# The place one-hots of the last sort, made in eight one-input column instructions in place of two wide two-input ones

## What is computed

```
h = relu(layernorm(x))
x = x + relu(relu((h*(1+eps) + segment_sum(h[src], dst)) @ W1 + b1) @ W2 + b2)      # layer one
h = relu(layernorm(x))
x = x + h @ w_self.T + scatter_add over edges e, at row src[e], of h[dst[e]] @ W_rel[type[e]]   # layer two
```

## Time and profile before

| what | value |
|---|---|
| three runs | 1236.69 us median (1233.98 to 1239.51) |
| the profiled execution | 1234.93 us, its span 1233.1 us |
| busy, share of the span | PE 73%, DVE 58%, ACT 30%, POOL 68% |
| last sort beside sort 2's groups | 409 to 618 us after the span's start |
| groups 47 to 51, end of layer one's sums | 622 to 642 us |
| dense part and products, first gather of layer two | 642 to 692 us |

### The profile page before, as it was taken

One profiled execution on the slowest core, in us unless ns is written; L12 is line 12 of the kernel. 1 busy time (PEld: TensorE's weight loads), 2 busy tenths in 40 slices (PEclk: granted clock), 3 DMA queues, 4 the chain that ended last, 5 costly groups with the idle time before them and its releaser, 6 DMA issues.

```text
span 1233.1 us, 13150 instructions
## 1 busy us (share of the span) xinstructions
PE 897.0 (73%) x3799; PEld 571.9 (46%) x3799; DVE 718.0 (58%) x2165; ACT 372.5 (30%) x945; POOL 834.9 (68%) x833
## 2 busy tenths in 40 slices
PE   4777848978744899999959998965655655655654
PEld 2443424434312577777634433844444444444443
DVE  7896569857578899999935432833222323322331
ACT  7444314635300588888804432000000000000001
POOL 0177757778777777777740475777777777777772
PEclk9688878989986899999968999977777777677677
DMA  4443323433342334334333898212122122121224
GB/s 100 121 134 113 108 61 101 135 105 100 107 110 75 106 105 133 110 105 138 107 49 121 264 299 266 54 52 54 52 54 54 51 54 53 52 53 52 53 54 73
DMA packets 50307, 122.86 MB, mean 100 GB/s; under 512 B 16156, under 2 KB 27021, under 8 KB 47487
## 3 DMA queue, kind: packets, MB, share of 16 engines
q0 software_dynamic: 33088, 67.82, 21.8%
q1 hardware_dynamic: 16844, 52.62, 13.5%
q10 hardware_dynamic: 308, 1.60, 0.5%
HBM read 71.86 MB, written 50.10 MB: 99 GB/s over the span
## 4 chain that ended last, share of the span: by engine, by line
POOL 25%; issue 9%; PE 8%; SPq 4%; DVE 2%; DMA 2%; ACT 0%; POOLq 0%; DVEq 0%; ACTq 0%
POOL gathered L423 25%; SPq L382 4%; PE ps L999 3%; PE ps L1081 2%; DMA gathered<-z_table,row_of 1%; DVE spare L890 1%; PE ps L1058 1%; PE ps L1048 1%; PE ps L1095 0%; DMA z_table<-spare 0%; DMA gathered<-h_table,row_of 0%; PE ps L1003 0%; DVE x_sb L920 0%; ACT spare L519 0%; DVE stats L580 0%
## 5 line engine op out<-in xcount | busy, mean ns | idle before, releaser
L423 POOL DMA_INDIRECT gathered<-h_table,row_of x416 | 443.7, 1067 | 187.7 <-issue 120.1
L423 POOL DMA_INDIRECT gathered<-z_table,row_of x410 | 388.6, 948 | 190.4 <-issue 120.0
L999 PE MATMUL ps<-node_hot,gathered 128*128 128x250 f32 x820 | 279.7, 511 | 170.7 <-DMA gathered<-z_table,row_of 170.7
L806 DVE TENSOR_SCALAR node_hot<-iota_f,key_of 128x250 f32<-128x250 f32 x410 | 153.8, 379 | 294.3 <-PE ps L999 286.1
L999 PEld LDWEIGHTS ps<-node_hot,gathered 128*128 128x128 f32 x820 | 208.1, 262 | 242.1 <-issue 207.0
L1003 PE MATMUL ps<-node_hot,gathered 128*128 128x506 bf16 (+1 forms) x1248 | 243.8, 350 | 75.9 <-DMA gathered<-h_table,row_of 57.6
L1003 PEld LDWEIGHTS ps<-node_hot,gathered 128*128 128x128 bf16 x1248 | 126.5, 103 | 179.4 <-issue 112.1
L498 ACT ACTIVATE place_val_b<-place_hot,code_b 125x128 f16<-125x128 f16 x400 | 173.8, 520 | 100.5 <-DVE place_hot L733 100.3
L490 ACT ACTIVATE scratch<-scratch,code_b 125x208 f16<-125x208 f16 (+1 forms) x328 | 114.4, 430 | 177.3 <-DVE scratch L758 177.3
L545 ACT COPY spare<-ps 128x500 f32<-128x500 f32 (+1 forms) x7 | 3.1, 563 | 459.8 <-PE ps L999 459.8
L972 PE MATMUL ps<-scratch,place_val_a 125*128 125x410 f16 x400 | 138.3, 346 | 2.6 <-DVE scratch L743 2.4
(11 more groups left out here) (170 smaller groups left out, 541.8 us busy)
## 6 DMA issues: line engine op xcount, KB each, us to landing
z_table<-spare SPq DMA_DIRECT2D x50, 448.0 KB
z_table<-zeros_z SPq DMA_DIRECT2D x19, 896.0 KB
gathered<-h_table,row_of POOLq DMA_INDIRECT x416
gathered<-z_table,row_of POOLq DMA_INDIRECT x410, 2.5
z_table<-spare SPq DMA_DIRECT2D x50, 52.0 KB
z_table<-zeros_z SPq DMA_DIRECT2D x19, 104.0 KB
out<-x_sb SPq DMA_DIRECT2D x6, 224.0 KB
h_table<-gathered SPq DMA_DIRECT2D x1, 1092.0 KB
```

Of the source, the lines that this page charges most:

```text
L423: pool.indirect_dma_start(place if s == LAST else place.rearrange("p j d -> p (j d)"), None, z_table if s == LAST else h_table, bass.Indir ...
L806: V.tensor_scalar(node_hot_of[s][:, k % HOTS[s], :], (iota_f if s == LAST else iota_h)[:, 0:WIDE[s]], key_of[s][:, k:k + 1], None, ALU.is_ ...
L999: last = T.matmul(psf[:, bass.ds(offs[i], WIDE[s])], rows, node_hot_of[s][:, k % HOTS[s], :], start=False, stop=False, skip_group_check=True)
```

## The change

In the last sort alone, `place_hot` and `place_val_a` of a batch are no longer made by two wide instructions. A new array `place_code_a`, which takes the memory of `place_val_a` with each column contiguous, is made column by column on DVE: one tensor input (`iota_h`), two per-partition scalars (`place_f`, `code_f1`), `is_equal` then `mult`. Each raises `code_ready`. ACT scales that column, in place of the 0/1 one, by what is now the low code divided by the high code. PE reads `place_code_a` for its first matmul. In `rank_place` two instructions (lines 711 and 712) are replaced by five, with a reciprocal among them; the high code has its zero moved so that it can be divided by. `read_last` takes the place of `read_sorted`, with two more DVE instructions. In the diff below the first `sort_last` is ACT's, the second DVE's; the block `if s == LAST` stands in `rank_place`, ahead of lines 711 and 712. The sorts before, PE's and ACT's instruction counts, the gathers and all of layer two's other work stay.

```
+        place_code_a = place_val_a[:, :, :, :].rearrange("p u v b -> p u (v b)").rearrange("p u (b v) -> p u b v", b=BATCH)
+        place_f, code_f1 = src_i.bitcast(F32), dst_i.bitcast(F32)
...
+            def sort_last(batch, buf):
+                for i in range(BATCH):
+                    act.wait_ge(code_ready, batch * BATCH + i + 1)
+                    nc.scalar.activation(place_val_b[:, buf, i, :], place_code_a[:, buf, i, :], ACT.Copy,
+                                         scale=code_b[1][:, batch * BATCH + i:batch * BATCH + i + 1]).then_inc(val_ready, 1)
...
-                own(V.tensor_copy(place_h[l][:, cs], scr1))
+                own(V.tensor_copy(place_f[:, :] if s == LAST else place_h[l][:, cs], scr1))
...
+                if s == LAST:
+                    own(V.tensor_scalar(code_f1[:, :], scr0, HALF_CODE, None, ALU.is_ge))
+                    own(V.scalar_tensor_tensor(code_f1[:, :], scr0, -HALF_CODE, code_f1[:, :], ALU.add, ALU.add))
+                    own(V.tensor_scalar(scr1.bitcast(F32), scr1, -HALF_CODE, 1.0 / CODE, ALU.add, ALU.mult))
+                    own(V.reciprocal(code_b[1][:, :], code_f1[:, :]))
+                    own(V.tensor_tensor(code_b[1][:, :], code_b[1][:, :], scr1.bitcast(F32), ALU.mult))
+                    return
...
+            def sort_last(s, batch, buf):
+                dve.wait_ge(batch_used, batch + (BATCHES_BEFORE[s] + 1))
+                for i in range(BATCH):
+                    c = batch * BATCH + i
+                    V.tensor_scalar(place_code_a[:, buf, i, :], iota_h[0:EP, 0:P], place_f[:, c:c + 1], code_f1[:, c:c + 1],
+                                    ALU.is_equal, ALU.mult).then_inc(code_ready, 1)
+                for i in range(BATCH):
+                    c = batch * BATCH + i
+                    last = V.tensor_scalar(chunk_hot[:, buf, i, 0:CHUNKS[s]], iota_h[0:EP, 0:CHUNKS[s]],
+                                           chunk_f[1][:, c:c + 1], None, ALU.is_equal)
+                last.then_inc(batch_ready, 1)
+
+            def read_last():
+                w = CHUNKS[LAST]
+                above, value = (scratch[:, i * WIDEST:i * WIDEST + w] for i in (1, 2))
+                dve.wait_ge(batch_used, BATCH_BUFS + BATCHES_BEFORE[LAST] + COLS[LAST] // BATCH)
+                own(V.tensor_scalar(above, ps[:, 7, 0:w], 0.25, None, ALU.is_ge))
+                own(V.scalar_tensor_tensor(value, ps[:, 7, 0:w], 0.0, above, ALU.add, ALU.subtract))
+                V.tensor_scalar(s0[:, 0:w], value, HALF_CODE + 0.5, CODE, ALU.add, ALU.mult).then_inc(sorted_read, 1)
+                dve.wait_ge(sorted_read, LAST + 1)
...
-                    T.matmul(ps[:, 7, 0:w], place_val_a[:, buf, :, i], hot, start=False, stop=False, skip_group_check=True)
+                    T.matmul(ps[:, 7, 0:w], place_code_a[:, buf, i, :] if s == LAST else place_val_a[:, buf, :, i], hot, start=False, stop=False, skip_group_check=True)
```

More of the change, by code:

```diff
@@ L229, in build @@
         place_ready, pair_ready = sem("place_ready"), sem("pair_ready")
-        batch_ready = sem("batch_ready")
+        batch_ready, code_ready = sem("batch_ready"), sem("code_ready")
         val_ready, val_a_ready = sem("val_ready"), sem("val_a_ready")
@@ L499, in sort_batch @@
                                          scale=code_b[l][:, c0 + batch * BATCH + i:c0 + batch * BATCH + i + 1]).then_inc(val_ready, 1)
-            for s in range(1, NSORT):
-                batches_alone(s, sort_batch if s == LAST else sort_pair, 0, COLS[s] // BATCH)
+            for s in range(1, LAST):
+                batches_alone(s, sort_pair, 0, COLS[s] // BATCH)
+            def sort_last(batch, buf):
[3 more added lines that the diff above has]
+                                         scale=code_b[1][:, batch * BATCH + i:batch * BATCH + i + 1]).then_inc(val_ready, 1)
+            for b in range(COLS[LAST] // BATCH):
+                sort_last(b, (BATCHES_BEFORE[LAST] + b) % BATCH_BUFS)
             def z_odd_copies(tiles):
@@ L864, in _ @@
                     dve.wait_ge(nhot_used, CHUNKS_BEFORE[s - 1])
-                groups_beside(s - 1, node_hots, sort_batch if s == LAST else sort_pair)
+                groups_beside(s - 1, node_hots, sort_last if s == LAST else sort_pair)
                 if s == LAST:
-                    read_sorted(s)
+                    read_last()
                 else:
```

## The result

The changed kernel takes **1283.98 us**, median of three runs (1283.56 to 1284.23), against 1236.69 us: ratio 1.0382, 95% interval 1.0344 to 1.0419. The profiled execution took 1283.56 us, its span is 1281.8 us, 48.7 us longer than before. The direction was forecast; the 1253 us and the range up to 1264 were not large enough.

A forecast was written before the change was run, and what follows sets the result against it. DVE, PE and POOL almost level in the last sort, DVE setting the pace; DVE's 18.0 + 4.2 + 1.0 = 23.2 us, past 5.0 us of slack, moves the end +18.2: 1234.93 + 18.2 = 1253 us, range 1242 to 1264.

The forecast's parts named there:

- DVE's price of the change: Last sort: eight place instructions at 1.81 us replace two wide ones at 1.45, 50 batches, +18.0 us of DVE.
- the code preparation: DVE ahead of the first node one-hot: five instructions with a reciprocal replace lines 711 and 712, +4.2 us.
- The estimate from the Trainium skill: Place one-hots on DVE: 0.094 us each, 0.75 us for eight, saving 35 us; the forecast used the trace row instead.
- The 5.0 us of slack: End of layer one: DVE and PE may be 5.0 us later against POOL before the end moves.
- what follows from group 47: End of layer one: group 47 added at 648.2, group 51's gathers start then instead of 629.98, end moves +18.2 us.
- The forecast's own range: Main case, chance 0.80: 1244 to 1262 us, from reciprocal, landing, per-instruction price and interference.
- ACT and PE at 0: Last sort: ACT's 3.49 us and PE's 4.08 us a step are covered by DVE's 4.48, cost 0.
- POOL at 0: Gathers beside the last sort: most of 21.4 us lost to wide instructions may go, but credit 0, POOL waits for PE.
- rival C: Last sort: an unbroken run of one-input DVE instructions starves gathers; at a 1.35 us mean, 1273 us; chance 0.07.
- Its decision point, 1.217 us: Mean gather beside the last sort above which gather starvation decides the time: 1.092 + 18.2 / 146 us.

The follow-up runs named there:

- e2: Changed kernel with each batch's place and chunk one-hots in turns of one, nothing added or left out; 1254.66 us, ratio 1.0124.
- e4: Kernel before plus an unused tensor_reduce, 0.32 us of DVE, in each of the last sort's 50 batches; 1253.90 us, ratio 1.0121.
- e9: Changed kernel with place and chunk one-hots in turns of two; 1269.57 us, ratio 1.0228.
- e7: Changed kernel with place and chunk one-hots in turns of four; 1277.48 us, ratio 1.0320.
- e3: Changed kernel with DVE waiting for its own signal once a batch, behind the eight place one-hots; 1265.42 us, ratio 1.0211.
- e5: Changed kernel with a small POOL memset ahead of each of sort 2's gathers, to move their phase; one run, 1290.43 us.
- e8: Kernel before with a next-group node one-hot after every two pair one-hots in sorts 1 and 2, last sort unchanged; 1218.34 us, ratio 0.9831.

## Why the prediction was right and wrong

- **DVE's price of the change: right.** Eight place one-hots take 504.48 - 502.70 = 1.78 us (forecast 1.81, removed 1.45); the step is 4.45 us (about 4.48). By these steps, DVE's cost is 50 x (4.45 - 4.12) = 16.5 us, not 18.0; in e2, where DVE is the bound throughout, first to last batch takes 222.6 us in place of 202.7, so 19.8 us. The 18.0 lies between. DVE's timeline ahead of the sort has the code preparation:

```profile
407.11 0.37 DVE L725 TENSOR_SCALAR dst_i<-t 125x400 f32<-125x400 int32 x1
407.51 0.61 DVE L726 SCALAR_TENSOR_TENSOR dst_i<-t,dst_i 125x400 f32<-125x400 int32 x1
408.15 0.49 DVE L727 TENSOR_SCALAR t<-t 125x400 f32<-125x400 int32 x1
408.68 2.65 DVE L728 RECIPROCAL code_b<-dst_i 125x400 f32<-125x400 f32 x1
411.37 0.57 DVE L729 TENSOR_TENSOR code_b<-code_b,t 125x400 f32<-125x400 f32 x1
411.98 0.87 DVE L849 TENSOR_SCALAR node_hot<-iota_h,key_of 128x250 bf16<-128x250 f16 x4
```

  411.98 - 407.11 = 4.87 us in place of 0.68: +4.2, as forecast. The estimate from the Trainium skill, "VectorE: DVE Perf Modes", section "The TRN2 errata — SBUF-src ops pay a fixed extra latency per instruction", 0.094 us for a place instruction, was far too low: 0.22 measured.
- **The 5.0 us of slack and what follows from group 47: right**, shown by e4 (22.0 us of DVE move group 51's gathers by 16.4) and e2 (POOL waits for PE, gathers at 650.26 for 648.2).
- **The forecast's own range** does not add up: -1, -2, -2 and -3 below and +9 and +3 above 1253 give 1245 to 1265, not 1244 to 1262. Nothing hangs on it.
- **ACT and PE at 0: right.** ACT falls from 42 to 28 us of 50, with the columns contiguous; the granted clock is 1.00 from 450 to 550 us, and 0.95 from 550 to 620, where DVE and PE wait.
- **POOL at 0: this step failed.** "POOL gains only lead" was written because the wide two-input instructions were the only thing that I saw stop a gather. Mean gathers were to come down to near 1.0 us; they went up to 1.425. That the replacement could hold gathers longer than what it replaced was in the sum at nothing, and only in rival C. With this, POOL ends 144 x 0.333 = 48 us later, past the 18.2 us that DVE needs, so POOL decides alone. Where the order of DVE's instructions lets gathers in, the forecast's 1253 us appears (e2).
- **Rival C had the mechanism, at a chance of 0.07 and a mean of 1.35 us, 1273 us.** Its decision point, 1.217 us, held: mean gathers of 1.324, 1.378 and 1.430 us (e9, e7, the change, all 412 to 640 us) go with 1270, 1277 and 1284 us, while 1.022 leaves DVE the bound. The row that should have weighed more is in the earlier trace rows: 1.2 us lost to seven one-input instructions. I set it against narrower runs that cost gathers little, without knowing why they did. POOL's timeline of the kernel before has, beside the chunk one-hots that start at 482.35:

```profile
482.71 1.03 POOL L423 DMA_INDIRECT gathered<-h_table,row_of  x1 [0.30 <-issue]
```

  It comes to end 1.31 us into the run, a moment at which the changed kernel holds gathers, and is 0.09 us late; 33 gathers of the kernel before come to end 1.30 to 1.32 us into it, and none is later than that. So the calm beside these runs belonged to a step with the wide instructions and the pauses in it, and said nothing of a step without them. What I also left out is that a periodic DVE step and the gathers lock to each other (2.90 and 0.95 us in turn, step after step), so that a meeting that was rare before comes in every step.
- By the Trainium skill, "SBUF — State Buffer", section "Who interferes with whom", a one-input DVE instruction such as `tensor_scalar` can also hold the port pair that it shares with GpSimd, for the whole instruction. I had cited only that section's sentence on two inputs. The traces agree that a run of one-input instructions holds a gather, but not on for how long: 1.96 us, through eight instructions and four more, not one of 0.24 us. Whether these instructions take that pair no trace here shows.

**What stays open.** When a gather is held. In the changed kernel 61 gathers come to end inside the chunk one-hots: those 0.35 to 1.38 us into them are held, 36 in all, those up to 0.33 or from 1.49 us on are not, so the moment matters. In e3 such moments hold none, and in the kernel before none at 1.30 to 1.32 us, so a pause ahead of the run matters, or the wait for a semaphore that comes with it, and why is not known. What keeps long holds out of the kernel before, the wide instructions, the pause between them or the moment, was not separated. e5 was to move the phase and did not. 51 gathers of the changed kernel come to end in its runs of eight place one-hots and none is held there, while runs of four of them (e7) hold 22 of 50. Whether "kind" is the width, the number of scalars, the output's type or the program's line was not separated. Nor were the semaphores: each node one-hot waits for one and raises one, each place instruction raises one, and of eight chunk one-hots only the last does; a change of kind is also a change in these.

## What to carry to other kernels

When a wide VectorE instruction is split into a stream of short alike ones beside indirect DMAs issued by GpSimd, cost the stream's effect on the DMAs and not only its own time: look at the longest gather beside each existing run, ask what will end the run after the change, and compare the new mean with what the consumer allows. Try the instructions of different kinds in turn. It adds no instruction; one by one it was worth 29 us here (e2), and one after every two 20 us in the kernel before (e8). Two engines that each run periodically can lock to each other, and then a meeting that was rare in the old trace comes in every step.

## What the runs showed of the hardware

A gather of 0.945 us can be held for 1.96 us by DVE instructions of 0.24 us each, though each is followed by another at once; in e9 it ends 0.19, 0.20 or 0.27 us after the start of the first instruction of another kind, to within about 0.01 us (97 of 97). With turns of one instruction no gather was over 0.16 us late (e2), with turns of two about four in five were held, 97 of 124 (e9). A wide product with two SBUF inputs holds a gather to its end: the 33 gathers of the kernel before (410 to 612 us) that come to end inside it all end 0.05 to 0.07 us into the chunk one-hots behind it, 0.13 to 0.76 us late; gathers that start inside it, as in the earlier trace rows, are 0.47 us late. One pause of 0.12 us a step, ahead of the run, took all holding away in e3, and a like one did not in sort 2 of the kernel before. A second per-partition scalar makes a short instruction dearer: 125x128 with two scalars takes 0.223 us from start to start, 128x250 with one takes 0.195. ACT scales eight contiguous columns of 125x128 in 2.44 us and eight with a step of 8 elements in 3.49.
